# Hosting the second layer's queries and keys, and the first layer's last epilogue, inside the chunks of a two-layer graph attention kernel

## The chip, the cores and the metric

The kernel runs on one core of a Trainium2 chip. The core has TensorE (PE in the rows, with its weight loads as PEld), VectorE (DVE), ScalarE (ACT), GpSimd (POOL) and SyncE (SP), each with its own in-order queue of instructions. The metric is the device time of one execution in microseconds (us).

## The reference, cut to what matters

```python
h = jnp.maximum(_layernorm(x), 0.0)                    # x is 8192 x 128
wh = h @ W; e = wh @ a[:128] + (wh @ a[128:]).T        # layer 0: graph attention
e = jnp.where(adj > 0, leaky_relu(e, 0.2), NEG_BIG)    # adj is 8192 x 8192, int32
x = x + elu(softmax(e) @ wh)
h = jnp.maximum(_layernorm(x), 0.0)                    # layer 1: cosine attention
Qn, Kn = cos_normalize(h @ Wq.T), cos_normalize(h @ Wk.T)
att = softmax(jnp.where(adj > 0, Kn @ Qn.T, NEG))      # along the columns
x = x + 0.5 * (att @ h) + 0.5 * h                      # rows without a neighbour keep h
```

## The kernel before, in words

All operands of large products are split into a high and a low fp16 part, and each product is three matmuls (high x high, high x low, low x high; the tuple `parts`).

**Layer 0** goes over 8 chunks of 1024 target nodes (`chunk`), and in each over 32 units of 256 source nodes. For a unit SP loads 1 MB of the adjacency into one of 8 slots (L307), ACT turns it into a mask (`mask0`, L485), DVE makes the weights in two instructions (L930), and PE multiplies them with the values in 48 matmuls (L1239). The epilogue of a chunk runs within the next one: `denominators`, quotients (ACT, L525), elu, residual, moments, the layer norm of the next layer (ACT, L552), and `split` into fp16 parts (L869, L871). It has two DVE passes over 1024 columns with two tensors (L847, L850).

**What layer 1 needs first.** For each of 16 groups `g` of 512 nodes: `t2(g)` transposes h in 8 PE instructions (L1173); `copy_ht(g)` moves the result to `q_buf` on DVE (L881); `qk(g)` makes queries and keys of the group in 12 matmuls (L1192), only for their norms; `square(g)` squares them on ACT (L593); `half_sums(g)` on POOL adds the halves (L431, groups 0 to 13); `norm_sums(g)` on DVE sums each vector (L947). From the sums `guess` (DVE, 3 instructions) and `factors` (POOL, 15 instructions) make inverse square roots, over three ranges of the 64 tiles (`FOLDS`). `transpose_factors`, `copy_rows` and two DMAs spread the key factors of 512 keys over all partitions; `keys(i)` (L1214), `key_scaled` (L971), `key_high` (L597) and `key_low` (L975) make the keys of chunk `i`.

In the kernel before, `t2(0)` to `t2(6)` and `qk(0)` to `qk(4)` stand in the last chunk of layer 0, and most of the rest stands between the layers, with the epilogue of chunk 7 of layer 0; `qk(14)`, `qk(15)` and `keys(1)` stand in the first chunk of layer 1.

**Layer 1** goes over 16 chunks of 512 keys, and in each over 16 units `n` of 512 queries. PE makes the scores in two halves of 6 matmuls (`scores`, L1286), ACT takes exponentials in two halves (`exps`, L632), DVE masks them (`mask`, L1022), ACT makes the high part (`high_part`, L638), DVE the low part (`low_part`, L1027), and PE multiplies with h in 40 matmuls (`values`, L1302 and L1307), three units behind the scores (`LAG`). Scores of unit n+1 wait, half by half, for the exponentials of unit n, since both have the same four banks. The order within an engine is the order of the code; steps in dictionaries `parts`, `ahead`, `late` and `early` are called after, before, or around the unit that is their key, and (g, k) means unit 4g + k.

## Time and profile before

| | us |
|---|---|
| median of 3 runs | 2183.47 |
| lowest and highest run | 2181.06, 2183.75 |
| profiled execution, its own time | 2182.64 |
| its span in the trace | 2180.9 |
| PE busy | 2140.9 (98%) |
| DVE busy | 1969.0 (90%) |
| ACT busy | 1746.0 (80%) |
| POOL busy | 69.1 (3%) |

The time is 1.74 us longer than the span. The page's view of 40 slices shows PE at nine tenths or more in all but a few: the first, and one near the middle. In that slice POOL has its second spell of work and the DMA engines nearly stop. It is the passage from layer 0 to layer 1, from about 750 to 825 us.

### The profile page before, as it was taken

The page shows a single profiled execution, that of the slowest core. Times are in us where ns is not written, and L with a number is a line of the kernel's source. Part 1 is how long each engine was busy: PE and PEld are TensorE (multiplying, and loading weights), DVE is VectorE, ACT ScalarE, POOL GpSimd, SP SyncE. Part 2 cuts the span into 40 slices and gives each one's busy share as a digit, 9 for nine tenths or more (in the row PEclk, how much of TensorE's full clock was granted, in tenths as well). Part 3 has the DMA queues.
Part 4 walks back from the last instruction along what each step waited for, and adds up shares of the span by engine and source line. Part 5 has one row for each costly group of instructions (what it writes and reads, how often), then busy time and mean ns, then how long its engine had stood idle before and what let it go on. Part 6 is the DMA issues. An engine that isn't in the chain of part 4 may idle for free.

```text
span 2180.9 us, 63003 instructions
## 1 busy us (share of the span) xinstructions
PE 2140.9 (98%) x26185; PEld 1733.6 (79%) x26185; DVE 1969.0 (90%) x1691; ACT 1746.0 (80%) x1917; POOL 69.1 (3%) x86
## 2 busy tenths in 40 slices
PE   5999999999999979999999999999999999999998
PEld 5999999999999967777777777777777777777776
DVE  7999999999999969889889889898898898898987
ACT  6687778777887668888888888888888888888886
POOL 1000000000000054000000000000000000000000
PEclk9999999999999999999999999999999999999999
DMA  6899999999999915666665665665665656656653
GB/s 249 331 379 405 386 405 398 398 405 401 399 401 387 378 56 207 209 212 215 206 217 198 209 226 197 212 215 198 221 216 194 221 204 211 213 194 222 215 194 115
DMA packets 153735, 573.57 MB, mean 263 GB/s; under 512 B 9936, under 2 KB 10576, under 8 KB 153168
## 3 DMA queue, kind: packets, MB, share of 16 engines
q1 hardware_dynamic: 142176, 546.02, 68.5%
q10 hardware_dynamic: 11376, 24.91, 3.0%
q8 instruction: 140, 2.29, 0.4%
q14 instruction: 43, 0.35, 0.0%
HBM read 558.24 MB, written 12.65 MB: 262 GB/s over the span
## 4 chain that ended last, share of the span: by engine, by line
PE 96%; DVE 3%; ACT 1%; issue 0%; DMA 0%; POOL 0%; ACTq 0%; DVEq 0%
PE bank L1239 32%; PE bank L1286 30%; PE bank L1307 21%; PE bank L1302 10%; PE bank L1192 1%; DVE hl_buf L745 1%; PE bank L1214 0%; DVE hl_buf L733 0%; PE bank L1133 0%; DVE q_buf L881 0%; DMA q_buf<-x 0%; ACT ring L632 0%; PE bank L1173 0%; DVE ab_col L947 0%; ACT hl_buf L552 0%
## 5 line engine op out<-in xcount | busy, mean ns | idle before, releaser
L632 ACT ACTIVATE ring<-bank,th_col 128x512 f32<-128x512 f32 x1024 | 648.2, 684 | 234.5 <-PE bank L1286 227.4
L1022 DVE SCALAR_TENSOR_TENSOR ring<-ring 128x2048 f32<-128x2048 int32 x256 | 586.7, 2292 | 151.9 <-ACT ring L632 151.8
L1239 PE MATMUL bank<-v_buf,ring 128*128 128x129 f16 (+1 forms) x12288 | 712.2, 220 | 6.5 <-DVE ring L930 6.2
L1239 PEld LDWEIGHTS bank<-v_buf,ring 128*128 128x128 f16 x12288 | 707.6, 98 | 10.2 <-issue 9.4
L1286 PE MATMUL bank<-v_buf,q_buf 128*128 128x512 f16 x3072 | 706.5, 380 | 3.2 <-ACT ring L632 2.4
L1307 PE MATMUL bank<-u_buf,hl_buf 128*128 (+2 forms) x8192 | 704.3, 220 | 0.0
L1307 PEld LDWEIGHTS bank<-u_buf,hl_buf 128*128 128x128 f16 x8192 | 631.8, 98 | 55.8
L930 DVE SCALAR_TENSOR_TENSOR ring<-r_ring,th_word,ring 128x1024 f32<-128x1024 f32 x512 | 620.8, 1280 | 19.8 <-ACT ring L485 19.5
L1027 DVE TENSOR_TENSOR hl_buf<-ring,hl_buf 128x2048 f16<-128x2048 f32 x256 | 584.9, 2285 | 0.7 <-ACT hl_buf L638 0.7
L1302 PE MATMUL bank<-u_buf,hl_buf 128*128 (+1 forms) x2048 | 557.9, 272 | 0.5 <-DVE hl_buf L1027 0.5
L485 ACT ACTIVATE ring<-ring 128x2048 f32<-128x2048 int32 x256 | 481.1, 1908 | 88.4 <-DMA ring<-adj 84.9
L1286 PEld LDWEIGHTS bank<-v_buf,q_buf 128*128 (+1 forms) x3072 | 291.0, 98 | 311.3 <-ACT ring L632 3.8
L638 ACT ACTIVATE hl_buf<-ring 128x2048 f16<-128x2048 f32 x256 | 488.7, 1909 | 0.6 <-DVE ring L1022 0.6
L1302 PEld LDWEIGHTS bank<-u_buf,hl_buf 128*128 128x128 f16 x2048 | 197.0, 96 | 30.5 <-DVE hl_buf L1027 0.7
L431 POOL TENSOR_TENSOR hl_buf<-hl_buf 128x512 f32<-128x512 f32 x14 | 19.1, 1368 | 570.9 <-ACT hl_buf L593 568.6
L552 ACT ACTIVATE hl_buf<-q_buf,nbias,rstd 128x128 f32<-128x128 f32 x64 | 25.6, 482 | 9.9 <-DVE nbias L724 9.8
L1192 PE MATMUL bank<-wqk_sb,q_buf 128*128 128x256 f16 x192 | 24.4, 279 | 8.2 <-DVE q_buf L881 5.3
L500 ACT ACTIVATE v_buf<-hl_buf 128x516 f16<-128x516 f32 x16 | 10.1, 638 | 25.0 <-DVE hl_buf L821 25.0
L593 ACT ACTIVATE hl_buf<-bank 128x1024 f32<-128x1024 f32 x14 | 14.2, 1024 | 18.2 <-PE bank L1192 18.2
L1192 PEld LDWEIGHTS bank<-wqk_sb,q_buf 128*128 128x128 f16 x192 | 18.4, 100 | 12.0 <-DVE q_buf L881 7.6
L648 ACT ACTIVATE r_ring<-bank,den 128x128 f32<-128x128 f32 x64 | 18.3, 377 | 6.6 <-DVE den L1044 6.6
L525 ACT ACTIVATE hl_buf<-bank,den 128x128 f32<-128x128 f32 x64 | 17.4, 383 | 7.0 <-DVE den L838 6.9
(145 smaller groups left out, 465.7 us busy)
## 6 DMA issues: line engine op xcount, KB each, us to landing
ring<-adj SPq DMA_DIRECT2D x512, 1024.0 KB, 5.5
r_ring<-a_rows SPq DMA_DIRECT2D x8, 512.0 KB, 7.1
x_dram<-q_buf ACTq DMA_DIRECT2D x8, 512.0 KB, 7.0
...
```

The costliest lines, as they stand in the source:

```text
L485: nc.scalar.activation(slot(k), slot(k, I32), ACT.Sign).then_inc(s_sg, 1)
L552: ins = nc.scalar.activation(h_buf[:, it * P:(it + 1) * P], xs[:, bass.ds(c * C0 + it * P, P)], ACT.Relu, bias=nbias[:, it:it + 1], scale= ...
L632: ins = nc.scalar.activation(p_ring[:, k, (2 * hf + m) * IW:(2 * hf + m + 1) * IW], bank[:, 2 * hf + m, :], ACT.Exp, scale=q_scale[:, j:j ...
L638: nc.scalar.activation(hl_buf[:, 0, k, :], p_ring[:, k, :], ACT.Copy).then_inc(s_ph, 1)
L930: ins = V.scalar_tensor_tensor(half, r_ring[:, par, :].rearrange("p (b n) -> p b n", b=2), th_word[:, 2 * u + jj:2 * u + jj + 1], half, AL ...
L1022: V.scalar_tensor_tensor(p_ring[:, k, :], adj_ring[:, k, :], 0.0, p_ring[:, k, :], ALU.is_gt, ALU.mult).then_inc(s_m, 1)
L1027: V.tensor_tensor(hl_buf[:, 1, k, :], p_ring[:, k, :], hl_buf[:, 0, k, :], ALU.subtract).then_inc(s_pl, 1)
L1192: ins = mm(qk_banks(g)[:, k * 2 * D:(k + 1) * 2 * D], q_buf[:, hs, g * IW + k * P:g * IW + (k + 1) * P], wqk16[:, ws, :], start=(x == 0), ...
L1239: ins = mm(acc0(par, it), weights0(k, ps)[:, it // 4, jj, f], v2[:, bass.ds((2 * j + us) * VW, D + 1)], start=False, stop=False, skip_grou ...
L1286: ins = mm(bank[:, 2 * hf + m, :], q_buf[:, qs, bass.ds(j * P, P)], k_buf[:, ks, bass.ds(i * IW, IW)], start=(x == 0), stop=(x == 2))
L1302: mm(acc1_wide(par, it), hl_buf[:, 0, k, f], v, start=head and m == 0, stop=False, skip_group_check=True)
L1307: ins = mm(o, hl_buf[:, ps, k, f], v.rearrange("p o c -> p (o c)"), start=False, stop=tail and m == 3 and (ps, us) == (1, 0), skip_group_c ...
```

## The change

PE gets every `t2` and `qk` of groups 0 to 11, the first `transpose_factors` and `keys(0)`, `keys(1)` within the units of layer 0's last chunk, and nothing stands between the layers. `t2(12)` and `t2(13)` stand between the two halves of the first scores, the rest within the first chunk of layer 1. The epilogue of layer 0's last chunk moves into the units of that same chunk of layer 1, with buffers of its own in `v_buf`. The quotients are split, three tiles first, so that one bank comes free early. POOL no longer adds halves: DVE sums 1024 columns for every group. The last 16 tiles' roots are made on DVE (`late_factors`, 15 instructions each for two ranges of 8 tiles), the first 48 on POOL in three ranges of 16. Key rows are written and read from ACT's queue; the keys are in a ring of two.

```diff
-EARLY = 5
-LATE = 14
-FOLDS = (0, 16, 56, T)
+EARLY = 12
+FOLDS = (0, 16, 32, 48, 56, T)
+POOL_FOLDS = 3
+LATE_STEPS = 12
...
-            for g in range(LATE):
-                half_sums(g)
-                if g == EARLY - 1:
-                    factors(0)
-            factors(1)
-            factors(2)
+            for b in range(POOL_FOLDS):
+                factors(b)
...
+            def square(g):
+                act.wait_ge(s_qk, g + 1)
+                if g == EARLY:
+                    act.wait_ge(s_lo, 2)
+                if g > 1:
+                    act.wait_ge(s_red, g - 1 if g < EARLY else g)
+                nc.scalar.activation(squares(g), qk_banks(g), ACT.Square).then_inc(s_sq, 1)
...
+                early = {8 + 2 * g: (lambda g=g: square(g)) for g in range(EARLY)} if c == NC0 - 1 else {}
+                keys_made = {22: lambda: rows_written(0), 24: lambda: load_factors(0, 2), 28: lambda: key_high(0),
+                             31: lambda: key_high(1)} if c == NC0 - 1 else {}
...
-                    ahead = {1: lambda: square(14), 4: lambda: square(15)}
-                    parts = {(0, 2): lambda: load_factors(1), (2, 2): lambda: key_high(1),
-                             (3, 1): lambda: load_factors(2), (3, 2): lambda: residual(0)}
+                    ahead = {6: lambda: square(12), 7: lambda: square(13), 11: lambda: square(14), 12: lambda: square(15)}
+                    parts = {(0, 0): other_quotients, (0, 1): exponential, (0, 3): x1_written, (1, 1): back_to_exp,
+                             (1, 2): lambda: normalised(0, 4), (1, 3): lambda: normalised(4, IT0),
+                             (2, 3): lambda: load_factors(2), (3, 2): lambda: residual(0)}
...
+                early = {4 + 2 * g: (lambda g=g: copy_ht(g)) for g in range(EARLY)} if last else {}
+                sums = {9 + 2 * g: (lambda g=g: norm_sums(g)) for g in range(EARLY)} if last else {}
+                keys_made = {15: lambda: guess(0), 20: lambda: copy_rows(0), 23: lambda: guess(1),
+                             26: lambda: key_scaled(0), 29: lambda: key_low(0), 30: lambda: key_scaled(1),
+                             31: lambda: key_low(1)} if last else {}
...
+                    parts = {(0, 0): negative, (0, 1): elu, (0, 2): residual, (0, 3): moments,
+                             (1, 0): lambda: (spread(), copies(12)), (1, 1): scales, (1, 2): lambda: norm_sums(12),
+                             (1, 3): lambda: norm_sums(13), (2, 0): split,
+                             (2, 1): lambda: (late_factors(3), copies(14)), (2, 3): lambda: norm_sums(14),
+                             (3, 0): lambda: (norm_sums(15), late_factors(4)),
+                             (3, 2): lambda: copy_rows(1)}
...
             def qk(g):
-                pe.wait_ge(s_hc, g + 1 if g < LATE else (g | 1) + 1)
+                pe.wait_ge(s_hc, g + 1 if g < EARLY else (g | 1) + 1)
...
+                    pe.wait_ge(s_nf, ROOT_STEPS * POOL_FOLDS)
+                    pe.wait_ge(s_lf, LATE_STEPS * (len(FOLDS) - 1 - POOL_FOLDS))
...
+                    for g in range(EARLY):
+                        early[2 + 2 * g] += ((t2, g),)
+                        early[6 + 2 * g] += ((qk, g),)
+                    early[19] += ((transpose_factors, 0),)
+                    early[23] += ((keys, 0),)
+                    early[29] += ((keys, 1),)
...
-                late = {0: ((qk, 14),), 3: ((qk, 15),), 7: ((keys, 1),), 10: ((transpose_factors, 2),)} if first else {}
+                late = {5: ((qk, 12),), 6: ((qk, 13),), 9: ((t2, 14), (t2, 15)), 10: ((qk, 14),), 11: ((qk, 15),),
+                        13: ((transpose_factors, 1),)} if first else {}
```

PE, the last chunk of layer 0. Before, units 24 to 26 have only their 48 products, and the first `qk` stands ahead of unit 27:

```order
L1239 MATMUL bank<-v_buf,ring 128x129 [waits weights_ready]
L1239 MATMUL bank<-v_buf,ring 128x129 x47
L1239 MATMUL bank<-v_buf,ring 128x129 [waits weights_ready]
L1239 MATMUL bank<-v_buf,ring 128x129 x47
L1239 MATMUL bank<-v_buf,ring 128x129 [waits weights_ready]
L1239 MATMUL bank<-v_buf,ring 128x129 x47
L1192 MATMUL bank<-wqk_sb,q_buf 128x256 [waits layer0_sums_read,weight_split_step,ht_copied]
L1192 MATMUL bank<-wqk_sb,q_buf 128x256 x11
```

With the change, around units 18 and 19 (the products are L1264, `qk` is L1207, `t2` L1194 and the transpose of the first key factors L1215):

```order
L1207 MATMUL bank<-wqk_sb,q_buf 128x256 [waits squares_ready,ht_copied]
L1207 MATMUL bank<-wqk_sb,q_buf 128x256 x11
L1194 MATMUL bank<-ident,u_buf 128x128 [waits ht_copied,epilogue0_vector]
L1194 MATMUL bank<-ident,u_buf 128x128 x7
L1264 MATMUL bank<-v_buf,ring 128x129 [waits weights_ready]
L1264 MATMUL bank<-v_buf,ring 128x129 x47
L1215 MATMUL bank<-ident,f_col 16x128 [waits norm_factors_step]
L1264 MATMUL bank<-v_buf,ring 128x129 [waits weights_ready]
L1264 MATMUL bank<-v_buf,ring 128x129 x47
```

A `qk` and a `t2` stand ahead of every second unit, and PE waits for POOL's factors ahead of unit 19.

DVE, the first chunk of layer 1, its first units. Before (L1022 masks, L1027 is the low part, L947 sums the squares):

```order
L1022 SCALAR_TENSOR_TENSOR ring<-ring 128x2048 [waits adj_in0,exp_ready]
L1022 SCALAR_TENSOR_TENSOR ring<-ring 128x2048 [waits adj_in1,exp_ready]
L1027 TENSOR_TENSOR hl_buf<-ring,hl_buf 128x2048 [waits high_ready]
L1022 SCALAR_TENSOR_TENSOR ring<-ring 128x2048 [waits adj_in2,exp_ready]
L1027 TENSOR_TENSOR hl_buf<-ring,hl_buf 128x2048 [waits high_ready]
L1022 SCALAR_TENSOR_TENSOR ring<-ring 128x2048 [waits adj_in3,exp_ready]
L1027 TENSOR_TENSOR hl_buf<-ring,hl_buf 128x2048 [waits high_ready]
L947 TENSOR_REDUCE ab_col<-r_ring 128x4x2 [waits squares_ready]
```

With the change (L1037 and L1042 are mask and low part, the rest is the epilogue of layer 0):

```order
L1037 SCALAR_TENSOR_TENSOR ring<-ring 128x2048 [waits adj_in0,exp_ready]
L863 TENSOR_SCALAR v_buf<-v_buf 128x1024 [waits layer0_sums_read]
L1037 SCALAR_TENSOR_TENSOR ring<-ring 128x2048 [waits adj_in1,exp_ready]
L1042 TENSOR_TENSOR hl_buf<-ring,hl_buf 128x2048 [waits high_ready]
L867 SCALAR_TENSOR_TENSOR v_buf<-v_buf 128x1024 [waits epilogue0_scalar]
L1037 SCALAR_TENSOR_TENSOR ring<-ring 128x2048 [waits adj_in2,exp_ready]
L1042 TENSOR_TENSOR hl_buf<-ring,hl_buf 128x2048 [waits high_ready]
L873 SCALAR_TENSOR_TENSOR v_buf<-v_buf,q_buf 128x1024 [waits epilogue0_vector]
L1037 SCALAR_TENSOR_TENSOR ring<-ring 128x2048 [waits adj_in3,exp_ready]
L1042 TENSOR_TENSOR hl_buf<-ring,hl_buf 128x2048 [waits high_ready]
L879 BN_STATS stats<-v_buf 128x6 [waits epilogue0_vector]
L879 BN_STATS stats<-v_buf 128x6 x7
```

Each unit now carries a step of the epilogue, and so it goes on to unit 12.

ACT, the first chunk of layer 1. Before, units 1 and 2 (L632 exponentials, L638 the high part, L593 a square):

```order
L632 ACTIVATE ring<-bank,th_col 128x512 [waits scores_ready]
L632 ACTIVATE ring<-bank,th_col 128x512
L593 ACTIVATE r_ring<-bank 128x1024 [waits qk_ready]
L638 ACTIVATE hl_buf<-ring 128x2048 [waits masked]
L632 ACTIVATE ring<-bank,th_col 128x512 [waits scores_ready]
L632 ACTIVATE ring<-bank,th_col 128x512
L632 ACTIVATE ring<-bank,th_col 128x512 [waits scores_ready]
L632 ACTIVATE ring<-bank,th_col 128x512
L638 ACTIVATE hl_buf<-ring 128x2048 [waits masked]
```

With the change, units 6 and 7 (L636 exponentials, L642 the high part, L559 the layer norm, L577 a square):

```order
L636 ACTIVATE ring<-bank,th_col 128x512 [waits scores_ready]
L636 ACTIVATE ring<-bank,th_col 128x512
L636 ACTIVATE ring<-bank,th_col 128x512 [waits scores_ready]
L636 ACTIVATE ring<-bank,th_col 128x512
L642 ACTIVATE hl_buf<-ring 128x2048 [waits masked]
L559 ACTIVATE v_buf<-v_buf,nbias,rstd 128x128 [waits epilogue0_vector]
L559 ACTIVATE v_buf<-v_buf,nbias,rstd 128x128 x3
L577 ACTIVATE r_ring<-bank 128x1024 [waits norm_sums_ready,qk_ready]
L636 ACTIVATE ring<-bank,th_col 128x512 [waits scores_ready]
L636 ACTIVATE ring<-bank,th_col 128x512
```

The square of group 13 waits for the sums of group 12 (`norm_sums_ready`), and the exponentials of unit 7 stand behind it.

## Rows read from the trace of the kernel before

**Rows 1.** Windows: us, busy PE, PEld, DVE, ACT, POOL, clock, DMA, GB/s

```profile
677.00:775.40 98.40, 98.40 (x1665) 97.71 (x1662) 85.78 (x97) 68.79 (x58) 7.31 (x8) 1.00 0.86 333
775.40:819.70 44.30, 32.89 (x244) 21.77 (x243) 32.71 (x54) 31.56 (x49) 29.83 (x37) 0.92 0.24 84
...
788.00:790.00 2.00, 2.00 (x14) 1.50 (x12) 1.64 (x5) 1.53 (x5) 1.30 (x1) 0.53 0.19 68
```

**Rows 2.** Timeline of PE: start, us, line, out<-in, count [idle before <-releaser]

```profile
738.00 1.06 PE L1173 MATMUL bank<-ident,u_buf 128*128 128x128 f16 x16
...
772.45 2.92 PE L1239 MATMUL bank<-v_buf,ring 128*128 128x129 f16 x48
775.21 1.47 PE L1192 MATMUL bank<-wqk_sb,q_buf 128*128 128x256 f16 x12
776.51 0.61 PE L1173 MATMUL bank<-ident,u_buf 128*128 128x128 f16 x8
...
787.63 2.30 PE L1192 MATMUL bank<-wqk_sb,q_buf 128*128 128x256 f16 x12 [2.98 <-DVE q_buf L881]
...
802.17 2.75 PE L1286 MATMUL bank<-v_buf,q_buf 128*128 128x512 f16 x12 [0.76 <-ACT hl_buf L593]
...
826.30 0.27 PE L1302 MATMUL bank<-u_buf,hl_buf 128*128 128x258 f16 x1
...
829.00 2.75 PE L1286 MATMUL bank<-v_buf,q_buf 128*128 128x512 f16 x12
831.59 0.27 PE L1302 MATMUL bank<-u_buf,hl_buf 128*128 128x258 f16 x1
...
887.93 0.81 PE L1214 MATMUL bank<-q_buf,m_sb 128*128 128x512 f16 x3
```

**Rows 3.** Timeline of DVE, last chunk of layer 0

```profile
700.67 1.23 DVE L850 SCALAR_TENSOR_TENSOR q_buf<-hl_buf,q_buf 128x1024 f32<-128x1024 f32 x1
...
704.21 1.64 DVE L856 BATCH_NORM_STATS2 stats<-q_buf 128x6 f32<-128x128 f32 x8
...
729.15 16.82 DVE L930 SCALAR_TENSOR_TENSOR ring<-r_ring,th_word,ring 128x1024 f32<-128x1024 f32 x14
...
748.29 0.67 DVE L881 COPY q_buf<-bank 128x1024 f16<-128x1024 f16 x1
748.89 4.86 DVE L930 SCALAR_TENSOR_TENSOR ring<-r_ring,th_word,ring 128x1024 f32<-128x1024 f32 x4
```

**Rows 4.** Timeline of DVE, first chunk of layer 1

```profile
837.50 1.22 DVE L947 TENSOR_REDUCE ab_col<-r_ring 128x8 f32<-128x1024 f32 x1
838.75 0.23 DVE L955 TENSOR_SCALAR ab_col<-ab_col,w_scale 128x16 f32<-128x16 f32 x1
839.01 0.17 DVE L957 TENSOR_SCALAR small<-ab_col 128x16 int32<-128x16 int32 x1
...
839.31 2.29 DVE L1022 SCALAR_TENSOR_TENSOR ring<-ring 128x2048 f32<-128x2048 int32 x1
841.51 2.28 DVE L1027 TENSOR_TENSOR hl_buf<-ring,hl_buf 128x2048 f16<-128x2048 f32 x1
```

**Rows 5.** Timeline of ACT, between the layers and in layer 1

```profile
776.13 2.18 ACT L525 ACTIVATE hl_buf<-bank,den 128x128 f32<-128x128 f32 x8 [1.39 <-DVE den L838]
...
788.60 3.19 ACT L552 ACTIVATE hl_buf<-q_buf,nbias,rstd 128x128 f32<-128x128 f32 x8 [0.47 <-DVE nbias L724]
...
811.38 1.03 ACT L593 ACTIVATE r_ring<-bank 128x1024 f32<-128x1024 f32 x1
...
835.78 2.56 ACT L632 ACTIVATE ring<-bank,th_col 128x512 f32<-128x512 f32 x4 [0.93 <-PE bank L1286]
838.24 1.91 ACT L638 ACTIVATE hl_buf<-ring 128x2048 f16<-128x2048 f32 x1
```

**Rows 6.** Timeline of POOL, first and second range of factors

```profile
774.97 0.24 POOL L412 TENSOR_TENSOR small<-small 128x32 f32<-128x32 f32 x1
...
814.35 2.31 POOL L421 TENSOR_TENSOR th_col<-small 128x40 f32<-128x40 f32 x1
```

370 lines of the change are left out of this document (176 added, 194 removed).

## The prediction, written before the changed kernel ran

> **What bounds the kernel now.** I read the windows first [rows 1]. In the last chunk of layer 0 PE is busy 98.40 of 98.40 us, and DVE 85.78. Between 775.4 and 819.7 PE is busy only 32.89 of 44.30 us, at a mean granted clock of 0.92. So PE bounds both layers, and the one place where it stands is the passage between them, which is what the change rewrites. Its size comes from PE's timeline [rows 2]. Prices, from start to start: one unit of layer 0 takes 2.76 (772.45 to 775.21), a `qk` 1.30, scores 2.59 (829.00 to 831.59), values 2.70 (826.30 to 829.00), a `t2` 0.45 (1.06 for two, less the overlap at the end). `keys` shows 0.81; scores show 2.75 and take 2.59, so less the same 0.16 it is 0.65. A transpose of factors I take at 0.1, half of the shortest differences here; it matters to nothing.
>
> Layer 0's products end at 775.21. The first chunk of layer 1 is over, with its 13th values, at 887.93, when `keys(2)` starts. Between lie 112.7 us. PE's work there is 16 scores (41.4), 13 values (35.1), 11 `qk` (14.3), 9 `t2` (4.0), 2 `keys` (1.3) and 2 transposes (0.2), together 96.4. So PE loses **16.3 us** before, and that is the ceiling of any gain. Part of it is the clock: after an idle time of 2.98 the `qk` at 787.63 takes 2.30 instead of 1.47, and the window 788 to 790 has a granted clock of 0.53, the lower of the two levels (1.2 GHz).
>
> **Layer 0's last chunk.** Seven more `qk` (9.1), five `t2` (2.3), two `keys` (1.3) and a transpose (0.1) move in: 12.8 us, the same work that leaves the passage, so this is neither gain nor loss. PE's products would end at 775.2 + 12.8 = 788.0, if nothing else is late. DVE gets twelve `copy_ht` instead of two, at 0.60 each (748.29 to 748.89), and twelve sums of 1024 columns at 1.2 [rows 3, 4], with two `guess` (0.65 each, as three short instructions), two `key_scaled` (0.6), two `key_low` (1.3) and a copy: 6.0 + 14.4 + 1.3 + 1.2 + 2.6 + 0.3 = 26 us. Added to 85.8 that is 112 of the chunk's 98.4 + 12.8 = 111 us. That looks as if DVE became the bound, but some of it falls after DVE's last weights, and DVE enters the chunk ahead and ended 15 us ahead before. The point to look at is its narrowest lead: DVE's unit 20 begins at 729.15 and its unit 22 is ready after six instructions of 1.21, at 736.4; PE wants it after the two `t2`, at 738.9. By unit 20 DVE has got 13 us more and PE 15 us more, so the lead stays at some 1 to 3 us and PE doesn't wait for weights. ACT's squares (0.93 of start to start, duration 1.03 [rows 5]) lie in its idle time.
>
> The first transpose of factors stands ahead of PE's unit 19 and waits for 15 instructions on POOL that start when DVE has done the sums of group 3 and `guess(0)`, after its unit 15. With DVE ahead by some 2 us and 2.2 us of sums and guess, that is about when PE starts unit 15. PE comes to unit 19 four units, two `qk` and two `t2` later: 14.5 us. Free, a POOL instruction takes 0.24 and follows the last after 0.33, so 15 take 5. Beside DVE's masks and low parts of 2.29 one took 2.31 [rows 6], that is, it waited out a whole DVE instruction. If each waited out one L930 of 1.21 they would take 15 x 1.3 = 19.5, and PE would stand 5 us. In 14.5 us DVE runs eight of those, for 9.7 us, and the rest of its time is copies, sums and waits: eight instructions at 1.3 and seven at 0.33 make 13 at the most, 11 if some slip in between. I take no stall, and keep 0 to 5 for the range. The Trainium skill ("SBUF — State Buffer", section "SBUF: two separate sides") says that GpSimd and a DVE instruction with two SBUF inputs shut each other out for a whole instruction; L930 has two such inputs, so by that rule alone it would be the 19.5 and the stall of 5. The trace agrees for the masks and low parts, with 2.31.
>
> **The first chunk of layer 1.** Here I walked the four queues, t = 0 at the end of layer 0. Prices are [rows 4, 5]: mask and low part 2.2 each, exponentials 1.24 a half (2.56 for both), high part 1.84, a sum 1.15 to 1.2, a dependent short instruction 0.21 to 0.26, the two-tensor passes of the epilogue 1.22, the moments 1.62, the eight quotients 0.27 each, the layer norm 3.2. The same walk over the kernel before, started at 802.17, ends the chunk at 888.3 where the trace has 887.93, so its prices are good.
>
> - PE begins at once with half of the scores and `t2(12)`, `t2(13)` (to 2.2), and the three first quotients are read by 1.6. No wait. But three units have no values, and scores wait for exponentials of the unit before: PE stands 4.6 us before the first values start at 15.7.
> - DVE's work up to the end of `late_factors(4)` is 13 masks and 12 low parts (25 x 2.21 = 55.3) and the hosted steps: negative 0.6 (one tensor in, taken like the copy), elu 1.2, residual 1.2, moments 1.6, variance 0.75, four copies 2.4, scales 0.35, four sums 4.7, split 1.9, twice 15 small steps at 0.2 (6.2): 20.9. Together 76 us, starting at 5.2. PE would want the second transpose of factors, which waits for that, at 4.6 + 73.0 = 77.6. DVE can't have it before 81.4. So **DVE becomes the bound of this chunk**.
> - It is worse than that, since DVE waits too. `qk(12)`, behind unit 5, waits for both copies, which stand behind mask 4, low part 3 and the variance: PE 28.9 to 32.8, 3.9 us. `square(13)` waits for `norm_sums(12)`, and the exponentials of unit 7 stand behind it, so DVE stands 43.8 to 47.4 for them; likewise `square(15)` and unit 12, 79.8 to 83.4. With four shorter waits DVE stands 10.6 us, and `late_factors(4)` ends at 92.0. PE stands 1.0 ahead of scores 9, 2.3 for the split ahead of `t2(14)`, 2.5 ahead of `qk(14)`, 4.7 for the transpose (87.4 to 92.1), 0.2 elsewhere.
> - After that come two scores and two values, 10.6: the 13th values end at 102.8. The check by sum: work 83.6 and waits 4.6 + 3.9 + 1.0 + 2.3 + 2.5 + 4.7 + 0.2 = 19.2.
>
> ACT has 4.4 of each 5.29 us unit from before and some 14 us more: 85 of 103, never the bound. From chunk 1 on the orders are the same, but for the write of the other key rows by ACT, 0.33 us. SP loses two waits of small DMAs, whose loads weren't late.
>
> **The sum.** Before 112.7; after 12.8 + 102.8 = 115.6: 2.9 us more. The clock: gaps of 1.4, 2.8 and 3.9 us stand ahead of PE work here, like the one of 2.98 before. The first slow spell would lie under DVE's delay, the second delays the scores of unit 6 and so the chain: 0 to 1.9, I take 1. Forecast 2180.9 + 3.9 = 2184.8 of span, and with the 1.74 around it 2186.5. The profiled execution (2182.64) lies 0.8 under the median of 2183.47, and I leave the number as it is: **2186.5**, 0.14% above the median, which is near the edge of what a measurement can tell (0.2%, 4.4 us).
>
> **Rivals.**
> - **DVE isn't held up** (faster): if squares and exponentials don't make DVE wait and it runs its 76.2 us from 5.2 without a gap, `late_factors(4)` ends at 81.4 and the chunk at 92.2. Then 12.8 + 92.2 is 7.7 less than before: 2175. For it: DVE has a backlog for most of the chunk. Against: the wait of `square(13)` is in the order of the queues. Chance 0.16.
> - **The passage is simply hosted** (faster): hosted steps cost nothing, and only the 4.6 of the start stays: 16.3 - 4.6 = 11.7 gained, 2171. DVE's sum speaks against it. Chance 0.04.
> - **POOL is shut out, or DVE's lead is gone in layer 0** (slower): 15 instructions at 1.3, PE stands ahead of unit 19 for 5 us, and the clock costs 1.9 instead of 1: 2186.5 + 5 + 0.9 = 2192.4. It decides from 0.95 us for a POOL instruction on, that is, as soon as DVE leaves it no room beyond its own ends. Chance 0.2.
> - **More waits behind the transitions than I found** (8 KB and 512 KB DMAs in layer 0's full queues hold ACT at unit 24, or a step of the epilogue comes late): up to 8 us, 2194. Chance 0.08.
>
> **How the numbers follow.** The forecast has 0.52, with times of 2181 to 2190: the bounds are a price error of 0.05 on 25 DVE passes (1.2), 0.5 on each late set of factors (2), and 0 to 1.9 for the clock. The range from 2174.5 to 2194.5 takes in all but the second rival and what is beyond the slower ones. Faster by over 0.2% (under 2179.1): 0.16 + 0.04 and nothing of the forecast: 0.2. Slower (over 2187.8): 0.28 and a third of the forecast: 0.45. Within: 0.35.
>
> **What would show it.** PE: L1264 and its guests end near 788, without idle time ahead of L1215; first values 15 to 16 us later; waits of PE for L908, for L898 and at the second transpose (L1220) for L948, of 2 to 5 us each; the chunk's end near 891 to 892. DVE: no idle of over 1.5 us in the chunk but two of some 3.6. POOL: the first 15 instructions in under 14 us. I am wrong if PE has under 10 us of waits in the chunk, if it waits for weights (L1020) in layer 0, or if L1215 waits.

## The result, and the profile after

| | before | after |
|---|---|---|
| median, us | 2182.80 (6 runs) | 2189.71 (6 runs) |
| lowest to highest | 2181.06 to 2183.75 | 2189.49 to 2192.54 |
| profiled execution, its span | 2182.64, 2180.9 | 2189.53, 2187.7 |

The changed kernel takes 1.0037 times the time of before, 95% interval 1.0026 to 1.0047: 6.9 us **slower**. That is 3.2 us over the forecast of 2186.5 and inside the range.

The windows answer to [rows 1]. The first is the whole first chunk of layer 1, up to its 13th values, and the others lie in it:

```profile
core 0: us, PE busy (x) PEld busy (x) DVE busy (x) ACT busy (x) POOL busy (x), PEclk, DMA share, GB/s
788.02:894.83 106.81, 91.85 (x797) 60.76 (x794) 85.63 (x93) 78.56 (x104) 2.06 (x9) 0.94 0.49 165
822.00:824.00 2.00, 2.00 (x7) 0.81 (x6) 2.00 (x2) 1.02 (x1) 0.00 (x0) 0.50 0.41 47
882.00:884.00 2.00, 1.38 (x4) 0.61 (x5) 1.96 (x4) 0.00 (x0) 0.00 (x0) 0.58 0.00 0
```

PE's timeline answers to [rows 2]. L1215 and L1220 are the two transposes of factors, L1304 scores, L1207 a `qk`, L1194 a `t2`, L1233 `keys`; the brackets show idle time and its releaser:

```profile
742.91 0.27 PE L1215 MATMUL bank<-ident,f_col 128*16 128x128 f32 x1
...
788.02 1.46 PE L1304 MATMUL bank<-v_buf,q_buf 128*128 128x512 f16 x6
...
800.53 4.37 PE L1304 MATMUL bank<-v_buf,q_buf 128*128 128x512 f16 x12 [2.29 <-ACT ring L636]
...
820.24 2.17 PE L1207 MATMUL bank<-wqk_sb,q_buf 128*128 128x256 f16 x12 [2.07 <-DVE q_buf L908]
...
822.20 3.79 PE L1304 MATMUL bank<-v_buf,q_buf 128*128 128x512 f16 x12
...
849.02 1.07 PE L1194 MATMUL bank<-ident,u_buf 128*128 128x128 f16 x16 [2.08 <-DVE u_buf L898]
...
857.60 2.00 PE L1207 MATMUL bank<-wqk_sb,q_buf 128*128 128x256 f16 x12 [2.23 <-DVE q_buf L908]
...
859.40 3.96 PE L1304 MATMUL bank<-v_buf,q_buf 128*128 128x512 f16 x12
...
882.62 0.39 PE L1220 MATMUL bank<-ident,f_col 128*64 128x128 f32 x1 [4.51 <-issue]
882.81 4.20 PE L1304 MATMUL bank<-v_buf,q_buf 128*128 128x512 f16 x12
...
894.83 0.81 PE L1233 MATMUL bank<-q_buf,m_sb 128*128 128x512 f16 x3
```

Three things are to be seen. Layer 0 ends where it was forecast, at 788.02, and PE doesn't wait ahead of L1215. The first chunk of layer 1 then takes 894.83 - 788.02 = 106.8 us; before, its end was at 887.93, so the end is 6.9 us later, and that is the whole result: from there to the end of the span it is 1292.9 us in the one kernel and 1293.0 in the other. And four times a wait of 2 to 4.5 us is followed by work in windows of 2 us whose granted clock lies between 0.50 and 0.60: scores that take 2.75 take 3.8 to 4.4. I call such a stretch a slow spell. PE's waits in the chunk add up to 14.9 us.

DVE's timeline and then ACT's, both of the changed kernel, show why PE waits (L1037 is the mask, L1042 the low part, L912 the sum, L577 the square, L948 the last step of `late_factors`):

```profile
831.74 1.21 DVE L912 TENSOR_REDUCE ab_col<-r_ring 128x8 f32<-128x1024 f32 x1
836.41 2.29 DVE L1037 SCALAR_TENSOR_TENSOR ring<-ring 128x2048 f32<-128x2048 int32 x1 [3.46 <-ACT ring L636]
...
873.78 2.29 DVE L1037 SCALAR_TENSOR_TENSOR ring<-ring 128x2048 f32<-128x2048 int32 x1 [3.46 <-ACT ring L636]
...
882.29 0.23 DVE L948 TENSOR_SCALAR f_col<-f_col,w_scale 128x8 f32<-128x8 f32 x1
```

```profile
833.04 1.02 ACT L577 ACTIVATE r_ring<-bank 128x1024 f32<-128x1024 f32 x1 [2.42 <-DVE ab_col L912]
...
870.41 1.02 ACT L577 ACTIVATE r_ring<-bank 128x1024 f32<-128x1024 f32 x1 [3.95 <-DVE ab_col L912]
```

These lines show how DVE comes to wait for its own sum. ACT's `square(13)` waits 2.42 us until DVE has summed group 12 (831.74 + 1.21); the exponentials of unit 7 stand behind the square; and DVE, which has nothing else in its queue ahead of the mask of unit 7, stands for 3.46 us. The same happens at unit 12. DVE's delay then reaches PE at the next step that needs DVE: L1194, L1207, L1220. The releaser "issue" at L1220 hides DVE: its `late_factors(4)` ends at 882.52 (882.29 + 0.23), and L1220 starts at 882.62.

### The profile page after: what moved, and what is told of

Its sections match the earlier page's. It is cut to its first block, busy times and chain, and to the rows that moved or that the text cites. A ratio compares the mean times of both kernels' runs of the same rounds, so it can differ in the third digit from the quotient of the medians.

```text
span 2187.7 us, 63005 instructions
## 1 busy us (share of the span) xinstructions
PE 2144.3 (98%) x26185; PEld 1734.7 (79%) x26185; DVE 1977.6 (90%) x1721; ACT 1741.2 (80%) x1913; POOL 36.0 (2%) x72
## 3 DMA queue, kind: packets, MB, share of 16 engines
q8 instruction: 140, 2.29, 0.4%
## 4 chain that ended last, share of the span: by engine, by line
PE 94%; DVE 4%; ACT 1%; issue 1%; DMA 0%; POOL 0%; ACTq 0%; DVEq 0%
PE bank L1264 33%; PE bank L1304 29%; PE bank L1325 20%; PE bank L1320 10%; PE bank L1207 1%; DVE hl_buf L1042 1%; DVE ring L1037 1%; DVE hl_buf L761 1%; PE bank L1233 0%; ACT ring L636 0%; DVE hl_buf L749 0%; PE bank L1194 0%; PE bank L1152 0%; DMA q_buf<-x 0%; DVE ring L1020 0%
## 5 line engine op out<-in xcount | busy, mean ns | idle before, releaser
L636 ACT ACTIVATE ring<-bank,th_col 128x512 f32<-128x512 f32 x1024 | 646.8, 684 | 234.8 <-PE bank L1304 226.7
L1037 DVE SCALAR_TENSOR_TENSOR ring<-ring 128x2048 f32<-128x2048 int32 x256 | 586.6, 2291 | 161.6 <-ACT ring L636 161.6
L1264 PE MATMUL bank<-v_buf,ring 128*128 128x129 f16 (+1 forms) x12288 | 714.0, 220 | 6.1 <-DVE ring L1020 5.8
L1264 PEld LDWEIGHTS bank<-v_buf,ring 128*128 128x128 f16 x12288 | 709.1, 98 | 9.7 <-issue 8.5
L1304 PE MATMUL bank<-v_buf,q_buf 128*128 128x512 f16 x3072 | 710.3, 381 | 4.1 <-ACT ring L636 4.0
L1020 DVE SCALAR_TENSOR_TENSOR ring<-r_ring,th_word,ring 128x1024 f32<-128x1024 f32 x512 | 621.7, 1283 | 19.0 <-ACT ring L474 18.9
L1042 DVE TENSOR_TENSOR hl_buf<-ring,hl_buf 128x2048 f16<-128x2048 f32 x256 | 584.8, 2285 | 0.0
L1320 PE MATMUL bank<-u_buf,hl_buf 128*128 (+1 forms) x2048 | 557.9, 272 | 0.5 <-DVE hl_buf L1042 0.5
L474 ACT ACTIVATE ring<-ring 128x2048 f32<-128x2048 int32 x256 | 480.7, 1908 | 81.4 <-DMA ring<-adj 78.0
L1304 PEld LDWEIGHTS bank<-v_buf,q_buf 128*128 (+1 forms) x3072 | 292.0, 98 | 315.5 <-issue 7.0
L642 ACT ACTIVATE hl_buf<-ring 128x2048 f16<-128x2048 f32 x256 | 488.9, 1910 | 0.6 <-DVE ring L1037 0.6
L1320 PEld LDWEIGHTS bank<-u_buf,hl_buf 128*128 128x128 f16 x2048 | 197.0, 96 | 30.5 <-DVE hl_buf L1042 0.7
L577 ACT ACTIVATE hl_buf<-bank 128x1024 f32<-128x1024 f32 x12 | 12.3, 1024 | 28.9 <-PE bank L1207 28.9
L559 ACT ACTIVATE hl_buf<-q_buf,nbias,rstd 128x128 f32<-128x128 f32 x56 | 22.4, 484 | 10.0 <-DVE nbias L740 10.0
L1207 PE MATMUL bank<-wqk_sb,q_buf 128*128 128x256 f16 x192 | 24.8, 281 | 4.3 <-DVE q_buf L908 4.3
L1207 PEld LDWEIGHTS bank<-wqk_sb,q_buf 128*128 128x128 f16 x192 | 18.4, 100 | 6.9 <-DVE q_buf L908 4.6
L1152 PE MATMUL bank<-hl_buf 128*128 128x130 f32 x128 | 18.5, 290 | 1.3 <-ACT hl_buf L440 1.3
L1152 PEld LDWEIGHTS bank<-hl_buf 128*128 128x128 f32 x128 | 16.5, 201 | 2.5 <-ACT hl_buf L440 1.5
```

The lines of the kernel that those rows point to most:

```text
L474: nc.scalar.activation(slot(k), slot(k, I32), ACT.Sign).then_inc(s_sg, 1)
L636: ins = nc.scalar.activation(p_ring[:, k, (2 * hf + m) * IW:(2 * hf + m + 1) * IW], bank[:, 2 * hf + m, :], ACT.Exp, scale=q_scale[:, j:j ...
L642: nc.scalar.activation(hl_buf[:, 0, k, :], p_ring[:, k, :], ACT.Copy).then_inc(s_ph, 1)
L1020: ins = V.scalar_tensor_tensor(half, r_ring[:, par, :].rearrange("p (b n) -> p b n", b=2), th_word[:, 2 * u + jj:2 * u + jj + 1], half, AL ...
L1037: V.scalar_tensor_tensor(p_ring[:, k, :], adj_ring[:, k, :], 0.0, p_ring[:, k, :], ALU.is_gt, ALU.mult).then_inc(s_m, 1)
L1042: V.tensor_tensor(hl_buf[:, 1, k, :], p_ring[:, k, :], hl_buf[:, 0, k, :], ALU.subtract).then_inc(s_pl, 1)
```

## The experiments

**The question.** Theory A, mine: the *order* of the hosted steps makes the queues wait for one another. Rival B: DVE's *amount* of work in this chunk is the bound, in whatever order it stands. And K: the slow clock behind the waits is what the sum lacked.

First the changed kernel and ten of the eleven variants of it, run 8 times each (the change 6 times, the first three reordered kernels 4, 5 and 3 times). The chunk's length is that from the first scores to L1233 in the profiled run. "Without spells" takes off what PE's slow spells behind `qk(12)`, `qk(14)` and L1220 add: from `qk(12)` to `qk(13)` it is 6.60 us at full clock, from `qk(14)` to `qk(15)` 6.61, and from L1220 behind unit 13 to L1233 10.68; what a trace shows above these is the spell. "Walk" is the prediction's 102.8 less what the run's expectation takes off, at full clock.

| kernel | median, us (range) | against before, 95% | chunk, us | without spells | walk, us |
|---|---|---|---|---|---|
| the change | 2189.71 (2189.49 to 2192.54) | 1.0026 to 1.0047 | 106.8 | 101.9 | 102.8 |
| transpose one unit later | 2184.54 (2182.97 to 2185.91) | 0.9999 to 1.0022 | 100.0 | 98.3 | 99.2 |
| second buffer for squares | 2182.31 (2179.99 to 2184.42) | 0.9990 to 1.0012 | 98.3 | 97.0 | 98.0 |
| sums one unit earlier | 2181.02 (2178.82 to 2182.93) | 0.9982 to 1.0004 | 99.1 | 95.7 | 96.8 |
| copies one unit earlier | 2186.81 (2186.07 to 2189.76) | 1.0011 to 1.0034 | 106.0 | 101.7 | 102.8 |
| one turn in `late_factors` | 2185.86 (2183.73 to 2186.81) | 1.0002 to 1.0023 | 101.0 | 99.4 | 100.3 to 100.8 |
| waits filled | 2184.93 (2184.72 to 2187.77) | 1.0004 to 1.0025 | 101.9 | 101.9 | 102.8 |
| **reordered** | **2172.22** (2172.02 to 2172.26) | 0.9936 to 0.9969 | 89.4 | 89.4 | 89.6 |
| reordered, one turn | 2172.95 (2172.07 to 2173.64) | 0.9945 to 0.9973 | 89.4 | 89.4 | 89.6 |
| reordered, second buffer | 2172.16 (2172.04 to 2172.56) | 0.9939 to 0.9971 | 89.4 | 89.4 | 89.6 |
| reordered, transpose at 13 | 2177.22 (2175.07 to 2178.02) | 0.9966 to 0.9987 | 94.0 | 92.3 | 92.6 |

Without the spells each of the single edits takes off what its walk said, within 0.5 us: 3.6 (walk 3.6), 4.9 (4.8), 6.2 (6.0), 0.2 (0), 2.5 (2.0 to 2.5). What the chunks of the profiled executions gain beyond that is slow spells. The medians rest on the other executions too, and these have no trace.

(The first transpose two units earlier is the eleventh run, told below.)

### One edit each on the changed kernel

**The transpose one unit later.**

```diff
-                        13: ((transpose_factors, 1),)} if first else {}
+                        14: ((transpose_factors, 1),)} if first else {}
```

> One edit to the changed kernel: PE's second transpose of factors (L1220) stands behind unit 14 of layer 1's first chunk instead of unit 13. In the changed kernel PE stands 4.5 us there, waiting for late_factors(4), and the chunk ends at 894.8 (13th values). Theory A (the hosted steps stand in an order in which the queues wait for one another; each wait is a loss of its own): a unit later PE has other work meanwhile, the wait goes and the chunk ends 3.6 us earlier, near 891.2; the kernel's time falls by 3.6, to 2186.0. Theory B (DVE has too much work in this chunk, and whatever order it stands in PE has to wait for it): the 4.5 us come back within two units, ahead of the next scores or values, and the time stays at 2189.5, within 1.

Measured: 5.2 us faster. The wait is gone:

```profile
881.80 0.27 PE L1220 MATMUL bank<-ident,f_col 128*64 128x128 f32 x1
...
885.55 0.28 PE L1320 MATMUL bank<-u_buf,hl_buf 128*128 128x258 f16 x1 [0.68 <-DVE hl_buf L1042]
```

Only 0.68 of the 4.51 us comes back, ahead of the next values (L1320). So PE had work of its own to do meanwhile, against B. The gain is 1.6 us over the forecast 3.6; the slow scores behind the wait (4.20 for 2.75) go with it, and they are 1.5 us.

**A second buffer for the squares**, so that `square(g)` waits for the sums of group g-2.

```diff
-            return sq_ring[:, g % 2, :] if g < EARLY else r_ring[:, 0, :]
+            return sq_ring[:, g % 2, :] if g < EARLY else r_ring[:, 0, :] if g % 2 == 0 else v_buf[:, 5 * C0:6 * C0]
...
-                    act.wait_ge(s_red, g - 1 if g < EARLY else g)
+                    act.wait_ge(s_red, g - 1)
```

> One edit to the changed kernel: the squares of groups 13 and 15 go to a free kilo-column of v_buf, so that ACT's square(13) and square(15) no longer wait for norm_sums(12) and norm_sums(14) on DVE. In the changed kernel each wait (2.4 and 4.0 us on ACT) holds back the exponentials of units 7 and 12, and DVE then stands 3.5 us twice. Theory A (the order makes the waits): both of DVE's idle times go or fall under 1 us, late_factors(4) ends some 5 us earlier, the wait ahead of L1220 goes, and the chunk ends 4.8 us earlier: 890.0, time 2184.7. Theory B (DVE's amount of work bounds the chunk): DVE's two idle times are the only slack it has, so removing them gains up to their 7 us as well, and it doesn't tell A from B; but a rival C, that these idle times of DVE lie beside PE's own work and cost nothing, says 0: 2189.5.

Measured: 7.4 us faster, where A said 4.8. C is out: the idle time of DVE ahead of units 7 and 12 falls from 3.46 to 0.97 each. PE's waits ahead of `t2(14)` and L1220 fall with it, from 2.08 to 0.68 and from 4.51 to 2.20; the one ahead of `qk(14)` stays at 2.23, so it has another cause, `late_factors(3)` and the copies in front of it.

**The sums one unit earlier.**

```diff
-                             (1, 0): lambda: (spread(), copies(12)), (1, 1): scales, (1, 2): lambda: norm_sums(12),
-                             (1, 3): lambda: norm_sums(13), (2, 0): split,
-                             (2, 1): lambda: (late_factors(3), copies(14)), (2, 3): lambda: norm_sums(14),
-                             (3, 0): lambda: (norm_sums(15), late_factors(4)),
+                             (1, 0): lambda: (spread(), copies(12)), (1, 1): lambda: (scales(), norm_sums(12)),
+                             (1, 2): lambda: norm_sums(13), (2, 0): split,
+                             (2, 1): lambda: (late_factors(3), copies(14)), (2, 2): lambda: norm_sums(14),
+                             (2, 3): lambda: norm_sums(15), (3, 0): lambda: late_factors(4),
```

> One edit to the changed kernel: DVE does norm_sums of groups 12 to 15 one unit earlier each (12 behind unit 5, 13 behind 6, 14 behind 10, 15 behind 11), and late_factors(4) alone behind unit 12. DVE has exactly the same instructions. Theory A (the order makes the waits): the sums are done before ACT comes to square(13) and square(15), DVE's two idle times of 3.5 us fall, and the chunk ends 6.0 us earlier: near 888.9, time 2183.5, as fast as the kernel before the change. Theory B (DVE's amount of work bounds the chunk, in any order): no more than 1 us, since DVE's work is the same: 2188.5 to 2189.5. C (the sums now wait for the squares themselves, because qk and squares of these groups aren't done a unit earlier): DVE stands ahead of L958, and the chunk gets longer by 1 to 3 us.

Measured: 8.7 us faster (A said 6.0, B at most 1) with exactly the same instructions on DVE. That alone refutes B, as far as the changed kernel goes. DVE's idle times at units 7 and 12 are 0.97 here too, and nowhere does L912 wait.

**The copies one unit earlier.**

```diff
-                    parts = {(0, 0): negative, (0, 1): elu, (0, 2): residual, (0, 3): moments,
-                             (1, 0): lambda: (spread(), copies(12)), (1, 1): scales, (1, 2): lambda: norm_sums(12),
+                    parts = {(0, 0): negative, (0, 1): elu, (0, 2): residual, (0, 3): lambda: (moments(), copies(12)),
+                             (1, 0): spread, (1, 1): scales, (1, 2): lambda: norm_sums(12),
```

> One edit to the changed kernel: the copies of transposed groups 12 and 13 (L908) stand behind unit 3 on DVE, behind the moments, instead of behind unit 4 and the variance. PE's qk(12), behind unit 5, waited 2.1 us for them. Theory A, by the walk through all four queues: the copies come earlier but the same steps are done ahead of unit 5's mask, and what PE gains ahead of qk(12) it loses at once, at the values and scores behind it, which wait for DVE's next low part: 0, within 1 us, 2189.5. Rival D (each wait of PE in the list of waits is worth its size): the chunk ends 2 to 3 us earlier, 2186.5 to 2187.5.

Measured: 2.9 us faster in the median, but 0.8 in the chunk of the profiled run. Neither theory has the median; without slow spells A's 0 holds (101.7 for 101.9). PE's rows show two effects:

```profile
833.43 2.76 PE L1304 MATMUL bank<-v_buf,q_buf 128*128 128x512 f16 x12 [1.86 <-ACT ring L636]
...
880.66 0.40 PE L1220 MATMUL bank<-ident,f_col 128*64 128x128 f32 x1 [4.52 <-issue]
880.85 5.33 PE L1304 MATMUL bank<-v_buf,q_buf 128*128 128x512 f16 x12
```

The wait of 2.07 for the copies turned into one of 1.86 two units later, as the walk said. But in its new place no slow spell followed it, which brought 2 us up to L1220 (880.66 for 882.62); and the slow spell behind L1220 came out longer in this execution, 5.33 for 4.20, and ate half of that. That the runs range over 3.7 us fits such spells, though only one of them has a trace.

**Only one turn in `late_factors`.**

```diff
-LATE_STEPS = 12
+LATE_STEPS = 6
...
-                for turn in range(3):
+                for turn in range(2, 3):
```

> The changed kernel with late_factors of 6 steps on DVE instead of 12 (only the last of three turns of the iteration, for the last 16 tiles; their norm factors are less exact, so that part of the computation is left out). It takes 2.0 us of small DVE steps out of the first chunk of layer 1, half of it before unit 10 and half before the second transpose of factors; nothing is moved. Theory A (the order makes the waits; DVE is held up by its own idle times behind ACT): the 1.0 us before L1220 is on PE's path in full, the 1.0 us before unit 10 is too, since DVE stands behind ACT only later, so 2.0 to 2.5 us: 2187.2 to 2187.7. Theory B (DVE's work is the bound everywhere): the same 2.0. Rival C (small steps fall into DVE's idle time of 2.8 us at unit 11): 1.0 or less, 2188.7. It gives the price of a small step on the path, to be held against the edits that only move steps.

This kernel leaves out two of the three turns of the iteration for the last 16 tiles. Measured: 3.9 us faster, for 2.5 us of small steps taken out. PE's waits ahead of `qk(14)` and L1220 fall by 1.26 each (0.97 and 3.25), which is the small steps one to one. The rest is slow spells: in the profiled execution, the fastest of the 8, none follows the waits ahead of `qk(12)` (1.98) and `qk(14)` (0.97). C is out. So in the changed kernel small DVE steps are on the path, as A and B both said.

**PE's waits filled with matmuls** that nobody reads. The waits' ends stay where DVE and ACT put them.

```diff
+                    if first and q in {3: 36, 9: 10}:
+                        pe.wait_ge(s_free, NC0)
+                        fill({3: 36, 9: 10}[q])
...
+                    if first and q in {5: 32, 9: 32, 10: 34, 13: 70}:
+                        fill({5: 32, 9: 32, 10: 34, 13: 70}[q])
```

> The changed kernel with 214 extra matmuls of 125 columns on PE in layer 1's first chunk, whose results nothing reads: 36 ahead of the scores of unit 3, 32 behind unit 5 (where PE waits for the copies), 10 ahead of the scores of unit 9, 32 behind unit 9, 34 behind unit 10, 70 behind unit 13. They fill PE's waits and nothing else; the waits stay as long as they were, in the order of steps. In the changed kernel four spells at a granted clock of 0.5 to 0.6 follow those waits, and PE's work in them takes 6.7 us more than at full clock. Theory K (the clock is the term missing from my sum, about 4 us on the path): with the waits filled the clock stays at 1.00 there, scores behind them take 2.75 instead of 3.8 to 4.4, and the chunk ends 3 to 4.5 us earlier, near 891: time 2185.5 to 2186.5. Rival (the slow spells lie beside DVE's work and cost nothing on the path, and the 4 us are prices of DVE's steps that I had too low): the clock is at 1.00 but the time stays at 2189.5, within 1, or grows by the extra matmuls where they are longer than the wait.

Measured: 4.8 us faster, with 214 matmuls more. The window of the chunk, of this kernel:

```profile
788.63:890.54 101.91, 97.13 (x1010) 70.73 (x1008) 85.52 (x93) 78.46 (x104) 2.05 (x8) 1.00 0.51 171
```

The clock is 1.00 for 0.94, DVE's busy time is the same 85.5, and the chunk takes 101.9 us for 106.8. Step by step the two kernels keep the same distances but for three: from `qk(12)` to `qk(13)` 8.28 us became 6.60, from `qk(14)` to `qk(15)` 8.29 became 6.61, and from L1220 to L1233 12.21 became 10.68. These three differences are 1.68 + 1.68 + 1.53 = 4.9 us. So **the slow clock behind the waits costs the changed kernel 4.9 us**, and K stands.

**The first transpose of factors two units earlier** in layer 0's last chunk, ahead of unit 17 (`early[17]` for `early[19]`).

> The changed kernel with PE's first transpose of factors (L1215) two units earlier in layer 0's last chunk, ahead of unit 17 instead of 19. POOL's 15 instructions end at 741.7 in the changed kernel, and PE would come to unit 17 near 735.6. Theory (the transpose waits for POOL alone, and POOL's time is fixed by DVE's instructions beside it): PE stands about 6 us ahead of L1215, layer 0's products end 6 us later, at 794, and the time is 2195.5. Rival (while PE stands, DVE runs ahead and PE gets the time back later, since DVE is busy 103 of 111 us of the chunk and PE waits for weights nowhere): layer 0 ends at 788 to 791 only if PE had waits to give back; there are none, so this would show as 2189.5 to 2192. A second rival (POOL is faster, as DVE stands still when its ring of weights is full, so POOL ends earlier than 741.7): 2190 to 2193.

Measured: 2198.22 (2 runs; 1.0052 to 1.0092), 8.5 us slower. PE's and POOL's rows of this kernel:

```profile
741.90 0.38 PE L1215 MATMUL bank<-ident,f_col 128*16 128x128 f32 x1 [5.95 <-POOL f_col L425]
742.07 4.69 PE L1264 MATMUL bank<-v_buf,ring 128*128 128x129 f16 x48
```

```profile
741.21 0.63 POOL L425 TENSOR_SCALAR f_col<-f_col,w_scale 128x16 f32<-128x16 f32 x1
```

The stall is 5.95 (forecast: about 6), POOL ends at the same time (741.8 for 741.7), and nothing is given back. On top comes the clock: the 48 products behind the stall take 4.69 instead of 2.91. The two make 7.7 of the 8.1 us by which layer 0 ends later (796.1 for 788.0). My expectation of 2195.5 had left the clock out again.

### The same steps in another order

If A holds, all the waits can be ordered away together.

```diff
-                    parts = {(0, 0): negative, (0, 1): elu, (0, 2): residual, (0, 3): moments,
-                             (1, 0): lambda: (spread(), copies(12)), (1, 1): scales, (1, 2): lambda: norm_sums(12),
-                             (1, 3): lambda: norm_sums(13), (2, 0): split,
-                             (2, 1): lambda: (late_factors(3), copies(14)), (2, 3): lambda: norm_sums(14),
-                             (3, 0): lambda: (norm_sums(15), late_factors(4)),
+                    parts = {(0, 0): negative, (0, 1): elu, (0, 2): lambda: (residual(), moments(), spread()),
+                             (0, 3): lambda: copies(12), (1, 0): scales, (1, 1): lambda: norm_sums(12),
+                             (1, 2): lambda: norm_sums(13), (1, 3): split, (2, 1): lambda: copies(14),
+                             (2, 2): lambda: (late_factors(3), norm_sums(14)), (2, 3): lambda: norm_sums(15),
+                             (3, 0): lambda: late_factors(4),
...
-                        13: ((transpose_factors, 1),)} if first else {}
+                        14: ((transpose_factors, 1),)} if first else {}
```

On ACT, `back_to_exp` stands behind unit 4 for 5.

> The changed kernel with the same steps in another order in layer 1's first chunk, nothing added or left out. DVE: residual, moments and variance together behind unit 2, copies 12 and 13 behind unit 3, scales behind 4, norm_sums(12) behind 5, norm_sums(13) behind 6, split behind 7, copies 14 and 15 behind 9, late_factors(3) and norm_sums(14) behind 10, norm_sums(15) behind 11, late_factors(4) behind 12. ACT: the table goes back to exponentials behind unit 4. PE: the second transpose of factors behind unit 14. Theory A (the order makes the waits, and the waits the loss): by the walk through the four queues the chunk ends 13.2 us earlier than with the changed kernel's order, at full clock; with the clock's part of the changed kernel (4 us too) gone or still there, the chunk ends at 877.7 to 881.6 and the time is 2173 to 2177, which is 6 to 10 us faster than the kernel before the change. Theory B (DVE's work in this chunk, 76 us of passes and small steps that start at 5, is the floor): late_factors(4) can't end before t = 81.4 after layer 0, so nothing below a chunk end of 880 to 881: 2175 to 2176 at best, and if passes are held up somewhere else, as one waits for something in any order, 2180. A chunk end above 886 refutes A.

Measured: 2172.22, 17.5 us under the changed kernel and 10.6 under the kernel before. The chunk ends at 877.53, just under A's 877.7 to 881.6 and 2.5 us under B's floor of 880. The window of the chunk, and PE's rows that had waits or slow scores in the changed kernel:

```profile
788.16:877.53 89.37, 84.61 (x796) 58.77 (x794) 82.79 (x91) 77.97 (x104) 2.06 (x9) 1.00 0.53 185
```

```profile
800.66 2.77 PE L1304 MATMUL bank<-v_buf,q_buf 128*128 128x512 f16 x12 [2.29 <-ACT ring L636]
...
815.10 0.28 PE L1320 MATMUL bank<-u_buf,hl_buf 128*128 128x258 f16 x1 [1.10 <-DVE hl_buf L1042]
...
872.13 0.27 PE L1220 MATMUL bank<-ident,f_col 128*64 128x128 f32 x1
872.24 2.75 PE L1304 MATMUL bank<-v_buf,q_buf 128*128 128x512 f16 x12
...
877.53 0.81 PE L1233 MATMUL bank<-q_buf,m_sb 128*128 128x512 f16 x3
```

PE's list of waits between 788 and 895, of this kernel and then of the changed one (us in total, times, longest):

```profile
PE bank L1304 <- ACT ring L636: 3.6, 3, 2.3
PE bank L1320 <- DVE hl_buf L1042: 1.1, 1, 1.1
```

```profile
PE bank L1220 <- issue: 4.5, 1, 4.5
PE bank L1207 <- DVE q_buf L908: 4.3, 2, 2.2
PE bank L1304 <- ACT ring L636: 4.0, 3, 2.3
PE bank L1194 <- DVE u_buf L898: 2.1, 1, 2.1
```

Every wait of PE ahead of a hosted step is gone. What stays is the start, where three units have no values yet (0.97 and 2.29 us, forecast as 4.6), the 1.10 us that the hosted steps make the low part late, and 0.34 us. DVE's waits in the chunk's masks fall from 19.9 us (9 of them) to 5.2 (2, both in the start).

**Does DVE bound the reordered kernel?** Its DVE is busy 80.1 of the 82.0 us from 796 on. Again with one turn in `late_factors` (P, in the expectation, is the theory that PE's own work and the chunk's start are now the bound):

> The reordered kernel with late_factors of 6 steps on DVE instead of 12, as in the run with one turn (two of three turns of the iteration for the last 16 tiles are left out). In the reordered kernel DVE runs from 796 to the chunk's end almost without idle time, 80.1 of 82.0 us, and PE is busy 78.3 of 82.0. Theory P (after the reordering PE's own work and the start of the chunk are the bound, DVE only keeps up): two microseconds less on DVE give nothing, by the walk through the queues 0.0: 2172.2, within 0.5. Theory B (DVE's amount of work bounds the chunk even now): 1.0 to 2.0 us faster, 2170.2 to 2171.2.

Measured: 2172.95, 0.7 above the reordered kernel and so 0.2 outside what P allowed, but on the slow side; in the profiled executions 0.6 of it lies ahead of the chunk (layer 0 ends at 788.78 for 788.16), and the chunk takes 89.4 us as before. The 2.5 us that gave 3.9 in the changed kernel give nothing here. P stands against B: a DVE that is busy 98% of the time, beside a PE that is busy 78.3 of these 82.0 us, isn't a bound as long as its results come in time.

**The second buffer on top.**

> The reordered kernel with the second buffer for the squares of groups 13 and 15. Alone, on the changed kernel, the buffer gave 7.4 us. Theory A (buffer and order take away the same wait, that of square(13) and square(15) for sums that come late): nothing is left for it, 2172.2, within 0.5. Rival (the buffer takes away a cost of its own, for instance DVE's sum and ACT's square colliding in one buffer): several us more, below 2170.

Measured: 2172.16. Buffer and order took away the same wait. The run shows something else, in PE's row at the chunk's start:

```profile
800.60 4.45 PE L1304 MATMUL bank<-v_buf,q_buf 128*128 128x512 f16 x12 [2.29 <-ACT ring L636]
```

These are the same scores behind the same 2.29 us of waiting as in the reordered kernel, at 4.45 us for 2.77, and the chunk takes 89.37 us in both. The reordered kernel's wait of 1.10 us for DVE ahead of L1320 is not there: the slow spell lies under DVE's delay and costs nothing.

**The transpose back at unit 13.**

> The reordered kernel with PE's second transpose of factors back behind unit 13, where the changed kernel has it. Theory A, by the walk through the queues: late_factors(4) ends some 3.0 us after PE comes to the transpose, so PE stands 3.0 us ahead of L1220; with the slow clock behind such a wait, up to 1.5 more: 2175.2 to 2176.7. Rival (DVE's order alone was the cause, the place of the transpose is of no account once DVE is early): 2172.2 to 2173.

Measured: 2177.22, 5.0 us slower than reordered and 0.5 above the top of A's forecast. The rows:

```profile
870.25 0.27 PE L1220 MATMUL bank<-ident,f_col 128*64 128x128 f32 x1 [2.81 <-issue]
870.36 4.44 PE L1304 MATMUL bank<-v_buf,q_buf 128*128 128x512 f16 x12
```

A wait of 2.8 us, and 1.7 of slow clock behind it. So the place on PE is a cause of its own, beside DVE's order. Of the other moves in the reordered kernel (the residual, the copies, the split, ACT's `back_to_exp`) none was tried alone on top of it.

## Why the prediction was right, point by point

- **The bound and its place.** Right: everything but the passage is unchanged (1292.9 us and 1293.0 behind it).
- **Layer 0's last chunk.** Forecast 788.0, measured 788.02. The work that moves in is neither gain nor loss, and DVE's lead held: PE has no wait for weights there in the trace.
- **POOL.** Forecast 11 to 13 us for the first 15 instructions, and eight of them held up; here is part of POOL's timeline, which answers to [rows 6]:

```profile
729.11 1.26 POOL L410 TENSOR_SCALAR ab_col<-ab_col 128x32 f32<-128x32 f32 x1 [522.46 <-DVE small L924]
730.45 1.04 POOL L413 TENSOR_TENSOR small<-small 128x32 f32<-128x32 f32 x1
731.57 0.25 POOL L415 TENSOR_TENSOR small<-small,ab_col 128x32 f32<-128x32 f32 x1
...
734.57 0.25 POOL L415 TENSOR_TENSOR small<-small,ab_col 128x32 f32<-128x32 f32 x1
...
741.09 0.64 POOL L425 TENSOR_SCALAR f_col<-f_col,w_scale 128x16 f32<-128x16 f32 x1
```

  They take 741.73 - 729.11 = 12.6 us, eight of them 1.0 to 1.3, the others 0.25 to 0.64. L415 is 0.25 at 731.57, beside DVE's copy from a bank, and at 734.57, beside DVE's sum; the long ones lie beside L1020, which reads two tensors. The Trainium skill ("SBUF — State Buffer", section "SBUF: two separate sides") names DVE instructions with two SBUF inputs as ones that shut out a GpSimd instruction that reads SBUF; the trace agrees, and 19.5 us would only come out if DVE had nothing else to do. L1215 had 1.2 us in hand (742.91 - 741.73), and the run with unit 17 shows what it costs when it hasn't.
- **The first chunk of layer 1, places.** Right: waits of PE of 2.1 ahead of `qk(12)`, 2.1 ahead of `t2(14)`, 2.2 ahead of `qk(14)` and 4.5 ahead of the transpose (forecast 3.9, 2.3, 2.5, 4.7), and DVE's two idle times of 3.46 (3.6). The first is short of its forecast since the slow scores of unit 3 bring PE there later: in the runs with the second buffer and with unit 17, where these scores are at full clock, it is 3.66. How much the places cost, without slow spells: the second buffer takes 2.5 us off each of DVE's two idle times and 4.9 off the chunk, of the 12.5 between the filled waits (101.9) and the reordered kernel (89.4). PE's transpose a unit early is worth 2.9 in the reordered kernel (92.3 for 89.4). The other 4.7 belong to the other moves together.
- **The first chunk, amount.** Forecast 102.8 at full clock; with the clock held at 1.00 by the filled waits it measures 101.9. So the walk was 0.9 too long: that term was off in the other direction.
- **"DVE becomes the bound of this chunk."** The arithmetic under this sentence held, the sentence didn't. It said that `late_factors(4)` can't end before 81.4 us into the chunk; in the reordered kernel, where DVE hardly waits, it ends at 81.6 (869.48 + 0.23 - 788.16). For a transpose behind unit 13 that is too late, and the last run shows the wait: 2.81 us. But it bounds only that one step. PE's transpose a unit later finds the factors ready, and PE then waits for DVE's 76 us of work only once, for 1.10 us, early in the chunk. So the changed kernel's 101.9 us at full clock were not DVE's work but the places of the steps: that was the part "It is worse than that, since DVE waits too". The rival "DVE isn't held up" was priced rightly for its transpose behind unit 13 (92.2; measured 92.3 without the spell), and with the transpose behind unit 14 the chunk gets nearer to the other rival, "simply hosted": 2172.2 for its 2171, which had a chance of 0.04.
- **The clock.** This is the term of the sum that was mis-sized: **1 us forecast, with 1.9 as its bound, and 4.9 measured** by filling the waits. I counted three gaps and took one of them as hidden; that part was right for the first (the run with the second buffer on top). But each of the other three waits, 2.07, 2.23 and 4.51 us long, had a slow spell behind it, of 1.6 to 1.7 us more work each. I had left the waits of 2.3, 2.5 and 4.7 of my own walk out of the count. The trace of before had shown the price too, in a row that I didn't read:

```profile
815.42 4.44 PE L1286 MATMUL bank<-v_buf,q_buf 128*128 128x512 f16 x12 [2.40 <-ACT ring L632]
```

  PE's work in the chunk measures 91.85 us for 84.61 in the reordered kernel at full clock: 7.2 us, a part of which only shortens waits that come after.
- **The signs.** POOL's 12.6 us, PE's 14.9 us of waits, and no wait for weights or ahead of L1215 came as written. Three did not: the first values start 16.7 us into the chunk (804.73) for 15 to 16, behind the slow scores of unit 3; the chunk ends at 894.83 for 891 to 892; and DVE has two more idle times over 1.5 us, 2.43 and 2.75, ahead of the masks of units 6 and 11. Those two stand behind the slow scores; with the waits filled they are 0.75 and 1.07. So DVE's rows show the missing term as well.
- **How much of the number was luck.** With 0.9 off the walk and 4.9 for the clock the sum comes to 2189.5 for the profiled execution, which measured 2189.53; that agreement is no test, since both corrections are read from the filled kernel against this one. With the walk as it was, the right price of the clock would have given 2190.4, just outside the 2181 to 2190 of the forecast's own band. The two errors partly cancelled.
